# Fifteen transposes of the identity ahead of TensorE's first real work

## The reference

```
h = max(layernorm(x), 0);  x = x + L0(h)    # GAT attention: softmax over leaky(s1_i + s2_j), masked by adj > 0
h = max(layernorm(x), 0);  x = x + L1(h)    # attention with scores (h*a_r) @ h.T, r chosen by adj in 1..4
h = max(layernorm(x), 0);  x = x + L2(h)    # sum over relations r of (adj == r) @ h @ W_r, plus bias
h = max(layernorm(x), 0);  x = x + L3(h)    # GAT attention with its own weights, then ELU
```

## Time and profile before

| | |
|---|---|
| median of 3 runs | 288.91 us |
| profiled execution | 288.16 us, span 286.3 us |
| TensorE (PE) busy | 273.2 us, 95% |
| VectorE (DVE) busy | 252.1 us, 88% |
| ScalarE (ACT) busy | 255.4 us, 89% |
| GpSimd (POOL) busy | 233.8 us, 82% |

### The profile page before, as it was taken

One profiled execution on the slowest core, in us unless ns is written; L12 is line 12 of the kernel. 1 busy time (PEld: TensorE's weight loads), 2 busy tenths in 40 slices (PEclk: granted clock), 3 DMA queues, 4 the chain that ended last, 5 costly groups with the idle time before them and its releaser, 6 DMA issues.

```text
span 286.3 us, 8109 instructions
## 1 busy us (share of the span) xinstructions
PE 273.2 (95%) x2250; PEld 256.9 (90%) x2250; DVE 252.1 (88%) x1217; ACT 255.4 (89%) x850; POOL 233.8 (82%) x376
## 2 busy tenths in 40 slices
PE   3899999999999999999999999999999999998991
PEld 1899998888889999999999999889889999998991
DVE  4799999988878887899999999998898888799985
ACT  5998988799998888999999999799999888796994
POOL 4899787777747999999999988887755799999722
PEclk9999999999999999999999999999999999999997
DMA  6955553400000000015343201000000000001213
GB/s 192 339 143 163 175 170 121 156 14 2 0 0 3 0 2 2 3 37 150 95 111 113 73 22 41 19 18 2 1 2 1 3 0 0 3 3 54 76 57 112
DMA packets 15949, 17.77 MB, mean 62 GB/s; under 512 B 2720, under 2 KB 11808, under 8 KB 15904
## 3 DMA queue, kind: packets, MB, share of 16 engines
q1 hardware_dynamic: 15488, 17.18, 19.2%
q10 hardware_dynamic: 416, 0.07, 0.1%
HBM read 13.05 MB, written 4.19 MB: 60 GB/s over the span
## 4 chain that ended last, share of the span: by engine, by line
PE 75%; DVE 14%; ACT 4%; issue 2%; POOL 2%; DMA 1%; SPq 1%; DVEq 0%
PE bank L1001 23%; PE bank L943 10%; PE bank L948 9%; PE bank L919 7%; PE bank L877 6%; PE bank L986 5%; PE bank L968 5%; DVE pT L700 4%; PE bank L956 4%; PE bank L998 3%; PE bank L950 2%; DVE st L625 2%; PE bank L903 2%; DVE mv L636 2%; DVE expy L736 1%
## 5 line engine op out<-in xcount | busy, mean ns | idle before, releaser
L367 POOL TENSOR_TENSOR rs<-mv,minus_half 128x2 f32<-128x2 f32 x128 | 89.7, 701 | 36.3 <-DVE mv L636 35.8
L1001 PE MATMUL bank<-val,pT 128*128 128x129 f32 x512 | 74.6, 275 | 0.0
L1001 PEld LDWEIGHTS bank<-val,pT 128*128 128x128 f32 x512 | 67.4, 192 | 0.0
L384 POOL TENSOR_TENSOR h<-h,rs 128x256 f32<-128x256 f32 x93 | 58.1, 625 | 2.3
L700 DVE SCALAR_TENSOR_TENSOR pT<-bank,val,edgesT 128x256 f32<-128x256 f32 x128 | 55.0, 471 | 0.8 <-PE bank L956 0.7
L625 DVE BATCH_NORM_STATS2 st<-x 128x6 f32<-128x128 f32 x192 | 45.2, 276 | 0.0
L528 ACT ACTIVATE val<-bank,val 128x128 f32<-128x128 f32 x128 | 44.3, 437 | 0.1
L636 DVE BATCH_NORM_AGGREGATE mv<-st 128x2 f32<-128x9 f32 x256 | 33.5, 172 | 10.8 <-DVE st L625 1.0
L877 PE MATMUL bank<-ident,h 128*128 128x128 f32 x192 | 38.0, 280 | 2.6 <-ACT hT L496 1.1
L376 POOL TENSOR_TENSOR h<-x,mv 128x256 f32<-128x256 f32 x64 | 40.0, 626 | 0.0
L919 PE MATMUL bank<-w_gat,hT 128*128 128x131 f32 x256 | 40.0, 279 | 0.0
(11 more groups left out here) (85 smaller groups left out, 661.0 us busy)
## 6 DMA issues: line engine op xcount, KB each, us to landing
edges<-in_adj SPq DMA_DIRECT2D x32, 256.0 KB, 3.0
xin<-in_x SPq DMA_DIRECT2D x32, 128.0 KB, 2.6
out_x<-result SPq DMA_DIRECT2D x32, 128.0 KB, 1.7
w_rel<-in_L_gnn_weight SPq DMA_DIRECT2D x1, 256.0 KB, 3.0
w_gat<-in_L_gnn_W ACTq DMA_DIRECT2D x1, 64.0 KB, 2.7
w_gat<-in_L_gnn_W SPq DMA_DIRECT2D x1, 64.0 KB, 3.4
a_rel<-in_L_gnn_a SPq DMA_DIRECT2D x4, 0.5 KB, 3.5
bias<-in_L_gnn_bias SPq DMA_DIRECT2D x1, 64.0 KB, 3.2
```

The costliest lines, as they stand in the source:

```text
L367: pool.tensor_tensor(rs[:, n % WIDE], mv[:, n % WIDE, :, 1], minus_half[:, :], ALU.pow).then_inc(rs_ready, 1)
L384: pool.tensor_tensor(h[:, n % HS, :, 0:D], h[:, n % HS, :, 0:D], rs[:, n % WIDE, :].rearrange("p (t o) -> p t o", o=1).to_broadcast([P, T, ...
L1001: last = pe.matmul(bank_o(n)[:, t], pT[:, n % 4, u, t * P:(t + 1) * P], values[:, u], start=(u == 0 and layer == 1), stop=(u == T - 1), sk ...
```

## The change

PE issues transposes of the identity into bank 7 at three places of the setup: eight ahead of `put_wT(0)`, three between it and `put_wa(0)`, four behind `put_wa(0)`. Nothing reads their result, they wait for no semaphore and signal none.

```
             pe.wait_ge(ident_ready, 9)
             ...
+            def spin(times):
+                for _ in range(times):
+                    pe.transpose(bank[7][:, 0:P], ident[:, :], ident[:, :])
+
+            spin(8)
             put_wT(0, ps_w)
+            spin(3)
             put_wa(0, ps_w)
+            spin(4)
```

## The result

The changed kernel takes 291.34 us (median of 6 runs, 290.38 to 292.91) against 288.62 us for the kernel before (288.35 to 289.55); the ratio is 1.0097, with an interval of [1.0069, 1.0125]. The forecast was 288.8, with a range that ended at 289.4. The profiled execution took 290.74 us with a span of 288.9, against 288.16 and 286.3 before: 2.6 us more in the span.

What follows compares the result with a forecast made beforehand. The prediction took x load, VectorE and GpSimd to set PE's entry at 13.07 us, with PE pacing the rest. Spins cost nothing and gain 0.1: 288.91 - 0.1 = 288.8 us, range 287.9 to 289.4.

Steps and rivals of the forecast that it cites:

- What bounds the kernel, and the front: Until 13.07 us x load, VectorE and GpSimd set PE's entry; only an earlier entry shortens the kernel.
- Costs of the three spins: Setup: overhang 0 for spin(8), 0.07 for spin(3), up to 0.55 for spin(4), inside the slack of 0.65; costs nothing.
- The 0.1 of gain: After 13.07 us: ACT running ahead may shorten an L919 group of 0.64; at least 0, at most 0.3, taken 0.1.
- The clock: PE's early rate: the rise to the fast rate comes near 6.5 us instead of 9.9, judged by durations.
- Nothing is removed or moved... no semaphore, no DMA, and no other engine touched: The fifteen transposes and their weight loads only add to PE's own stream; nothing else is affected.
- the unseen: Chance of 0.04 that the kernel gets slower by over 1.4 us for a reason no row shows.
- Slow rate costs in the timed runs: Rival: late clock rise delays PE's entry 1.4 us in timed runs; change gives 287.5, or 288.2 if half; chance 0.20.
- The overhang gets through: Rival: spins don't raise the clock and their overhang passes the slack ahead of 13.07; costs 0.4 us, 289.3; chance 0.10.
- ACT sets the pace: Rival: ACT limits the first units, so the 0.3 us it gets ahead is kept; 288.6; chance 0.05.
- the forecast's own range: Range of the main case, front chain untouched; -0.3 to +0.2, also given as 288.4 to 289.2; chance 0.65.

Runs made afterwards that it cites:

- e2: Changed kernel with PE's never-entered branch body for large weights emptied to a single wait; 288.15 us against 288.31, ratio 1.0005.
- e7: Changed kernel with the first eight transposes alone, spin(3) and spin(4) removed; one run, 291.13 us.
- e1: Kernel before with fifteen transposes placed inside PE's branch that is never entered; 290.85 us against 288.31, ratio 1.0077.
- e12: Kernel before plus six transposes behind PE's last real matmul; one time, 291.71 us.
- e8: Changed kernel with twenty transposes ahead instead of fifteen, spin(4) made spin(9); one run, 291.84 us.
- e3: Kernel before with the fifteen transposes behind PE's last real matmul instead of ahead; 288.52 us, ratio 1.0011.
- e4: Changed kernel plus 20 one-by-one matmuls (80 instructions) behind PE's last real matmul; 287.86 us, ratio 1.0001.
- e9: Changed kernel plus fifteen transposes behind PE's last real matmul; one run, 288.24 us.
- e6: Changed kernel plus one transpose behind PE's last real matmul; one run, 290.70 us.
- e10: Changed kernel plus six transposes behind PE's last real matmul; one run, 290.78 us.
- e14: Changed kernel plus fifteen transposes behind PE's last real matmul, second GAT layer's weights loaded behind the sixth x load, not the third; 287.71 us, ratio 0.9976.

## Why the prediction was wrong

*What bounds the kernel, and the front.* Right. The chain came in at 13.12 us, within the 13.0 to 13.1 that I had named but for 0.02, and the first half of the argument (a clock that rises early is worth nothing, because DMA, VectorE and GpSimd set the entry) stood its test in e2: 1.0005.

*Costs of the three spins.* Right in size. spin(8) at 0.22 was 1.76; the weights were released at 4.19 instead of 4.01, with the load landing later in this execution (PE was idle between the eighth spin and L856's weight load by 0.41 us of PEld), so no overhang came of it. L861 began at 5.10 (foreseen 4.89), the first transposes of h at 6.37 (foreseen 6.21), and PE had caught up at 7.47. ACT took the first hT at 6.94, as foreseen; what I had not seen is that PE's second transposes of h would wait for this (0.34 us of idle time), not for VectorE's h. They started at 7.47, where I had 7.42, and it came to nothing by 13 us. The 0.1 of gain didn't come either: the one L919 group of 0.64 us on the chain, from which I took it, is still there (L926 at 21.01).

*The clock.* Right: it rose near 6.7 us, foreseen 6.5, though that it came so near is partly luck. The durations and the first clock record of each trace put the rise at 5.2 to 8.1 us in the nine profiles with fifteen or more transposes ahead, at 9.2 to 13.9 in the six with none, and at 11.7 in e7, which has the first eight alone. The record of the kernel before begins at 9.9 us, with the rise, so the 1.00 that the earlier trace rows show for 5 to 7 us is no measurement of the clock; it was right to go by the durations. In the changed kernel PE ran 16 transposes and two matmuls before 6.37 us; the last group of these, spin(4) at 5.48, is still spaced by 0.22. The Trainium skill, "TensorE: Matmul & The Clock Gate", Part 4, says that transposes don't engage the full clock; these rows speak against it, as an almost pure stream of transposes moved the rise by 3 us.

*The step that failed* is "Nothing is removed or moved... no semaphore, no DMA, and no other engine touched". The instructions themselves are bytes that a DMA brings, and they move all that stands behind them. PE's stream ends in a jump over a body that never runs. I had looked for the loss in the time around the added instructions, took the stretch behind the flag as fixed (2.2 us of span behind the last work, none of it in my sum), and gave the unseen 0.04. The profile before had the row for it: PE's COMPARE_BRANCH at 365 ns, beside other engines' 45 to 72. The term is 3922 - 365 = 3.56 us, less 0.37 by which the flag came earlier in that pair of executions (0.33 of it time that PE lost between 169 and 183 us in the profile of before), less some 0.6 of what used to follow PE's branch on other engines and now lies beside it; the span shows 2.6, the medians 2.7. The Trainium skill, "Runtime: NRT & Kernel Launch", section "Instruction fetch mechanics", has the rule that I should have weighed: code comes in blocks of 16 KiB, fetched in sequence, and a taken branch to a block that isn't there waits for a DMA. The transfers of 16384 bytes on q8, the one that starts some 1 us after the branch in the changed kernel, and e1 agree with it. The page gives no price for the stall; here it is 3.2 to 3.7 us on PE's branch.

*The rivals.* "Slow rate costs in the timed runs" was to explain the spread. e1's and e12's profiled executions had the rise at 13.6 to 13.9 us and were 1.8 and 1.6 us late from the 100th matmul on. But e8's, with the spins and an early rise, was 1.7 late too, and what the three share is the x flight: 5.01, 4.73 and 5.24 us instead of 3.51. As far as these profiles tell, the lateness is mainly that load; the slow rate added about 0.3 in the two, where I had priced a rise at 13 us at 1.4. The timed runs have no trace, so what spreads them isn't shown. "The overhang gets through" was on the right side of zero with a wrong mechanism; no run shows it. "ACT sets the pace" left no trace in the times. (I gave the forecast's own range in two ways that differ, -0.3 to +0.2 and 288.4 to 289.2; nothing hangs on it.)

*What stays open:* why the next piece of code comes ahead of the branch with fifteen transposes or twenty small matmuls behind the last real work (e3, e4, e9), and not with one or six (e6, e10) or with five more spins at the front (e8). It isn't the number of instructions ahead of the branch alone: e3 has 30 more than the kernel before and gets it, e8 has 39 more and doesn't. In e3 the transfer even starts before the added transposes do.

## What to carry to other kernels

Instructions that are hidden in time still take room in their engine's code. If the stream ends in a branch over a body, even one that never runs, read that branch's duration in both profiles before you ask what an edit did; here it was worth 3.6 us, more than anything the edit aimed at, and it came and went with some fifteen instructions. The branch's row alone isn't enough, as e12 shows: compare the whole stretch from the last real work to the end, and in it each engine's rows of the closing barrier. Control for it: put the same instructions where they aren't run. And before an engine's clock or pace in the ramp-up is improved, find the row at which that engine enters the chain, since what comes to it from a load won't come sooner.

## What the runs showed of the hardware

A taken COMPARE_BRANCH on PE lasts 0.365 us (target loaded), 0.471 us (in e3, e4, e9 and e14, where one more piece had been fetched) or 3.6 to 4.0 us (target to be fetched), and in the seven profiles with such a branch the fetch starts about 1.0 us after it. In e12 a wait of 2.5 us of the same kind stood at PE's last instruction instead, behind a branch of 0.365 us. The flight of one and the same 128 KB load, issued at 4.02 us among others, was 3.14 (e4) to 5.24 us (e8) between executions of kernels that issue it alike, and PE entered the chain at 12.80 in the one and at 14.81 in the other. So one timed run of this kernel can't tell 1%, while the stretch from the flag to the end in one profile can: 2.2 us, or 4.8 and more. Two levels of PE's rate showed in the early durations, 0.22 and 0.11 us a transpose, while the granted clock was printed as 1.00, for lack of a record before the rise.
